# Short 32 by 32 blocks in four column strips of the tensor engine: a one-core block of attention, state-space convolution and low-rank feed-forward

## The reference

```python
def attention(h):                        # h = einsum('bct,bcd->bdt', x, W[condition])
    q, k, v = h @ Wq + bq, h @ Wk + bk, h @ Wv + bv          # 512 -> 4096
    q, k = rms_norm(q, gq), rms_norm(k, gk)                  # over all 4096
    # 32 heads of 128; the attention is within each batch of 32 tokens
    attn = softmax(einsum('bhqd,bhkd->bhqk', q, k) / sqrt(128))
    return einsum('bhqk,bhkd->bhqd', attn, v) @ Wo + bo
def ssm(u):                              # per token position (32 channels), over the 512 features
    K = 2 * einsum('hn,hnl->hl', Ct, exp(P)).real            # kernel of 512 taps for each channel
    y = irfft(rfft(u, 1024) * rfft(K, 1024))[..., :512] + u * D      # a causal convolution
    return y * (arange(512) < length)
def ffn(y):                              # 8 groups of 128 tokens, each with a gate over 16 adapters
    A_eff, B_eff = gate @ lora_A, gate @ lora_B              # rank 32, beside a shared pair
    return y @ kernel + bias + (y @ A_eff.T) @ B_eff.T + (y @ A_s.T) @ B_s.T
x = x + attention(mix(x));  return x + ffn(ssm(x))
```

## Time and profile before

| | |
|---|---|
| median of 3 runs | 891.25 us (889.63 to 892.67) |
| profiled execution | 890.15 us, its span 888.4 us |
| granted TensorE clock, mean over the span | 0.996 |
| TensorE matmuls busy | 97% of the span, 4,529 instructions |
| TensorE weight loads busy | 81% (beside the matmuls) |
| VectorE, GpSimd, ScalarE busy | 66%, 50%, 43% |

### The profile page before, as it was taken

One profiled execution on the slowest core, in us unless ns is written; L12 is line 12 of the kernel. 1 busy time (PEld: TensorE's weight loads), 2 busy tenths in 40 slices (PEclk: granted clock), 3 DMA queues, 4 the chain that ended last, 5 costly groups with the idle time before them and its releaser, 6 DMA issues.

```text
span 888.4 us, 12311 instructions
## 1 busy us (share of the span) xinstructions
PE 857.6 (97%) x4529; PEld 715.3 (81%) x4529; DVE 585.8 (66%) x641; ACT 378.5 (43%) x494; POOL 440.2 (50%) x429
## 2 busy tenths in 40 slices
PE   5799999999999999999799999999999999999988
PEld 4588888888888888888688888888888888888465
DVE  3977888887777777777856646566575766452421
ACT  3556555566555555564323214442321414132410
POOL 5989844432222222111999700469999995000500
PEclk9999999999999999999899999999999999999999
DMA  6125111111111111220011010131401011437301
GB/s 172 48 79 139 47 41 48 34 51 43 44 47 47 47 47 47 71 95 0 1 48 48 18 58 20 47 94 47 96 8 53 35 48 50 172 113 236 108 24 72
DMA packets 77473, 56.50 MB, mean 64 GB/s; under 512 B 25494, under 2 KB 60662, under 8 KB 77318
## 3 DMA queue, kind: packets, MB, share of 16 engines
q1 hardware_dynamic: 76480, 55.67, 20.8%
q10 hardware_dynamic: 966, 0.48, 0.2%
HBM read 52.32 MB, written 3.82 MB: 63 GB/s over the span
## 4 chain that ended last, share of the span: by engine, by line
PE 89%; POOL 5%; DVE 2%; ACT 1%; issue 1%; DMA 0%; ACTq 0%; POOLq 0%
PE psum L636 14%; PE psum L637 14%; PE psum L638 14%; PE psum L682 10%; PE psum L683 10%; PE psum L684 10%; PE psum L776 6%; PE psum L715 6%; PE psum L880 2%; PE psum L909 1%; PE psum L931 1%; POOL small L466 1%; POOL w_raw L401 1%; DVE wv_lo L1292 1%; POOL small L467 1%
## 5 line engine op out<-in xcount | busy, mean ns | idle before, releaser
L396 POOL TENSOR_TENSOR w_raw<-w_raw 128x256 f32<-128x256 f32 x32 | 26.7, 836 | 175.2 <-DMA w_raw<-in_wk 174.7
L1417 DVE TENSOR_TENSOR acc<-psum,acc 128x512 f32<-128x512 f32 x64 | 44.2, 691 | 96.0 <-PE psum L638 96.0
L682 PE MATMUL psum<-t_hi,w_hi 128*128 128x512 f32 x256 | 102.6, 401 | 1.9 <-DVE qk_sb L1259 0.9
L636 PE MATMUL psum<-wv_hi,mix_hi 128*128 128x512 f32 x256 | 100.3, 392 | 0.0
L683 PE MATMUL psum<-t_lo,w_hi 128*128 128x512 f32 x256 | 99.8, 390 | 0.0
L684 PE MATMUL psum<-t_hi,w_lo 128*128 128x512 f32 x256 | 99.7, 390 | 0.0
L637 PE MATMUL psum<-wv_lo,mix_hi 128*128 128x512 f32 x256 | 99.6, 389 | 0.0
L638 PE MATMUL psum<-wv_hi,mix_lo 128*128 128x512 f32 x256 | 99.6, 389 | 0.0
L1092 ACT ACTIVATE attn_hi<-psum,params 128x512 fp32r<-128x512 f32 x64 | 43.6, 688 | 116.5 <-PE psum L776 116.1
L636 PE MATMUL psum<-wo_hi,attn_hi 128*128 128x512 f32 x224 | 87.1, 389 | 0.0
L637 PE MATMUL psum<-wo_lo,attn_hi 128*128 128x512 f32 x224 | 87.1, 389 | 0.0
(11 more groups left out here) (237 smaller groups left out, 1915.4 us busy)
## 6 DMA issues: line engine op xcount, KB each, us to landing
w_raw<-in_wq SPq DMA_DIRECT2D x32, 256.0 KB, 2.9
w_raw<-in_wk SPq DMA_DIRECT2D x32, 256.0 KB, 3.2
wv_raw<-in_wv SPq DMA_DIRECT2D x8, 1024.0 KB, 5.4
toep<-kpad_dram SPq DMA_DIRECT2D x2, 4096.0 KB, 14.5
wo_raw<-in_wo SPq DMA_DIRECT2D x7, 1024.0 KB, 5.3
x_nat<-in_x SPq DMA_DIRECT2D x4, 512.0 KB, 6.0
acc<-in_x SPq DMA_DIRECT2D x1, 2048.0 KB, 10.0
out_dram<-o_stage SPq DMA_DIRECT2D x8, 256.0 KB, 2.0
```

The lines of the kernel that those rows point to most:

```text
L636: mm(out, lh, rh, start=(n == 0), stop=False)
L682: mm(bank(n), wh, hi[:, c, tok], start=(i == 0), stop=False)
L1417: v.tensor_tensor(acc[:, g, :], bank(6 + g % 2), acc[:, g, :], ALU.add).then_inc(acc_ok, 1)
```

## The change

1. The scores of a head become 32 matmuls of 32x32 instead of 8 of 128x128. Batch b of a group runs in column strip b of the array and lands on partitions 32b to 32b+31 of one half bank. `extract` becomes one copy of 128x256.
2. The second quad's value weights get tiles of their own (`wv_hi1`, `wv_lo1`). ScalarE splits them after the fifth group's copy and no longer waits for the value products; GpSimd's tables wait for sixteen value groups (`v_mm`, 2G) and no longer for `p_ok`.
3. The kernel generation goes in four strips (channel 8q+i in strip q) into one bank. The copy to `k_sb`, the load of D, the addition of D and the writing to `kpad` each become four pieces, and the addition also waits for the first half of `mix_lora`.
4. The last output weights are split before the last attend: ScalarE's high part when all value products are done, VectorE's remainder within quad 6, after the fifth accumulation.
5. The down product runs per group in two strips of 64 columns, waits for `y_t` and the adapters alone, and no longer makes the unused halves. Its result and `b_all` are split, and the up product is three f32r matmuls. ScalarE makes `y_t` ahead of `y_hi` in the last unit. GpSimd's zeroing moves behind the fourth convolution unit.

```diff
             for g in range(G):
-                last = mm(bank(6, 1024)[:, P * g:P * g + P], qk_sb[:, slot, 0, P * g:P * g + P],
-                          qk_sb[:, slot, 1, P * g:P * g + P], start=True, stop=True)
+                for b in range(BPG):
+                    tok = slice(P * g + SEQ * b, P * g + SEQ * b + SEQ)
+                    last = mm(bank(6)[quadrant(b), SEQ * g:SEQ * g + SEQ], qk_sb[:, slot, 0, tok],
+                              qk_sb[:, slot, 1, tok], start=True, stop=True, tile_position=(0, 32 * b))
...
-                for b in range(BPG):
-                    src = bank(6, 1024)[quadrant(b), :].rearrange("p (g k) -> p g k", g=G)[:, :, quadrant(b)]
-                    last = sc.activation(dst[quadrant(b), :].rearrange("p (g k) -> p g k", g=G), src, ACT.Copy)
-                last.then_inc(s_ok, 1)
+                sc.activation(dst, bank(6, G * 32), ACT.Copy).then_inc(s_ok, 1)
...
-            pool.wait_ge(p_ok, 1)
+            pool.wait_ge(v_mm, 2 * G)
...
-                value_group(1, g)
+                value_group(1, g, hi=wv_hi1, lo=wv_lo1)
...
-            for g in range(4, G):
+            value_out(0, 4)
+            act.wait_ge(wv1_in, 16)
+            sc.activation(wv_hi1[:].rearrange("p c n -> p (c n)"), wv_raw1[:].rearrange("p c n -> p (c n)"),
+                          ACT.Copy).then_inc(wvhi_ok, 1)
+            for g in range(5, G):
                 value_out(0, g)
-            act.wait_ge(wv1_in, 16)
-            act.wait_ge(v_mm, G)
-            sc.activation(wv_hi[:].rearrange("p c n -> p (c n)"), wv_raw1[:].rearrange("p c n -> p (c n)"),
-                          ACT.Copy).then_inc(wvhi_ok, 1)
...
-            split_v(1, raw=wv_raw1)
+            split_v(1, raw=wv_raw1, hi=wv_hi1, lo=wv_lo1)
...
-                last = mm(bank(0, 1024)[0:CA, CL * h:CL * h + CL], u_tab[:, :, h], expo[:, 0:CL, h],
-                          start=True, stop=True)
+                i, q = h // 4, h % 4
+                last = mm(bank(0)[32 * q:32 * q + CA, CL * i:CL * i + CL], u_tab[:, :, 8 * q + i], expo[:, 0:CL, 8 * q + i],
+                          start=True, stop=True, tile_position=(0, 32 * q))
...
-            gp.tensor_tensor(k_sb[:, :, CL - 1], k_sb[:, :, CL - 1], d_rows[:], ALU.add).then_inc(kern_d, 1)
+            pool.wait_ge(lora, 2 * NLORA - 1)
+            for q in range(4):
+                rows = slice(32 * q, 32 * q + CA)
+                gp.tensor_tensor(k_sb[rows, :, CL - 1], k_sb[rows, :, CL - 1], d_rows[rows, :], ALU.add).then_inc(kern_d, 1)
+                pool.wait_ge(kern_d, q + 1)
...
-            gp.memset(ax[:], 0.0).then_inc(ax_zero, 1)
...
+            pool.wait_ge(conv_mm, 4)
+            for tile in (ax_hi, ax_lo):
+                gp.memset(tile[:].bitcast(F32), 0.0).then_inc(ax_zero, 1)
...
-            attn_out(NQ - 1, range(4))
+            act.wait_ge(v_mm, G * NQ)
             split_o(NQ - 1, hi=wv_hi, raw=wv_raw)
-            attn_out(NQ - 1, range(4, 8))
+            attn_out(NQ - 1)
...
                     accumulate(t, (3 + c,), first)
+                    if c == 1 and not split:
+                        split_o(t + 1, hi=wv_hi, lo=wv_lo, raw=wv_raw)
...
             pe.wait_ge(yt_ok, 8)
-            pe.wait_ge(ylo_ok, 8)
             pe.wait_ge(a_in, 16)
             for j in range(G // 2):
-                down(j)
+                for c in range(KC):
+                    for k in range(2):
+                        g = 2 * j + k
+                        last = mm(bank(0)[2 * RANK * k:2 * RANK * k + 2 * RANK, P * j:P * j + P], a_all[:, c, g, :],
+                                  y_t[:, c, BPG * g:BPG * g + BPG, :], start=(c == 0), stop=(c == KC - 1),
+                                  tile_position=(0, 64 * k))
+            last.then_inc(ax_mm, 1)
+            pe.wait_ge(ylo_ok, 8)
...
-                pe.wait_ge(ax_ok, g + 1)
+                if g < 2:
+                    pe.wait_ge(axlo_ok, g + 1)
                 if g == 0:
-                    pe.wait_ge(b_in, 64)
-                mm(o, ax[:, g, :], b_all[:, g // 2, :], start=False, stop=True).then_inc(out_mm, 1)
+                    pe.wait_ge(blo_ok, 1)
+                mm(o, ax_hi[:, g, :], b_hi[:, g // 2, :], start=False, stop=False)
+                mm(o, ax_hi[:, g, :], b_lo[:, g // 2, :], start=False, stop=False)
+                mm(o, ax_lo[:, g, :], b_hi[:, g // 2, :], start=False, stop=True).then_inc(out_mm, 1)
...
+                if u == 3:
+                    act.wait_ge(b_in, 64)
+                    sc.activation(b_hi[:].rearrange("p j n -> p (j n)"), b_all[:].rearrange("p j n -> p (j n)"),
+                                  ACT.Copy).then_inc(bhi_ok, 1)
+
+            def half_groups(tile, k):
+
+                return tile[2 * RANK * k:2 * RANK * k + 2 * RANK].rearrange("p (j k) t -> p k j t", k=2)[:, k]
+
+            def low_rank(k):
+
+                return bank(0)[2 * RANK * k:2 * RANK * k + 2 * RANK, :].rearrange("p (j t) -> p j t", j=G // 2)
+
+            act.wait_ge(ax_mm, 1)
+            act.wait_ge(ax_zero, 2)
+            for k in range(2):
+                sc.activation(half_groups(ax_hi, k), low_rank(k), ACT.Copy).then_inc(axhi_ok, 1)
...
+                if u == 5:
+                    dve.wait_ge(bhi_ok, 1)
+                    v.tensor_tensor(b_lo[:].rearrange("p j n -> p (j n)"), b_all[:].rearrange("p j n -> p (j n)"),
+                                    b_hi[:].rearrange("p j n -> p (j n)").bitcast(F32), ALU.subtract).then_inc(blo_ok, 1)
             y_low(7)
...
+            for k in range(2):
+                rows = slice(2 * RANK * k, 2 * RANK * k + 2 * RANK)
+                dve.wait_ge(axhi_ok, k + 1)
+                v.tensor_tensor(ax_lo[rows].rearrange("p (j k) t -> p k j t", k=2)[:, k],
+                                bank(0)[rows, :].rearrange("p (j t) -> p j t", j=G // 2),
+                                ax_hi[rows].rearrange("p (j k) t -> p k j t", k=2)[:, k].bitcast(F32),
+                                ALU.subtract).then_inc(axlo_ok, 1)
```

More of the change, by code:

```diff
@@ L149, in build_program @@
          (wo_raw, _, wv_raw),
-         (_, wv_raw1),
+         (_, wv_hi1, wv_raw1),
+         (_, wv_lo1),
          (_, ang, expo, mult, quarter, quarter_pi),
@@ L155, in build_program @@
          (t_hi, t_lo, w_raw0, w_hi0, w_lo0, w_raw1, w_hi1, w_lo1, qk_sb, sq, sumsq, bo_rows),
-         (ffn_lo, ffn_hi, a_all, b_all, ax, fb_rows, mask, _, x2p, y_t, y_hi, y_lo),
+         (_, b_lo),
+         (ffn_lo, ffn_hi, a_all, b_all, _, fb_rows, mask, b_hi, x2p, y_t, y_hi, y_lo),
          (wo_lo, wo_hi, _, wv_lo, wv_hi, v_sb, p_blocks, attn_hi, attn_lo)) = overlay(
@@ L170, in build_program @@
              ("bo_rows", [P, FEAT], F32)],
+            [gap(24), ("b_lo", [P, G // 2, FEAT], F32R)],
             [("ffn_lo", [P, KC, FEAT], F32R), ("ffn_hi", [P, KC, FEAT], F32R), ("a_all", [P, KC, G, 2 * RANK], F32),
-             ("b_all", [P, G // 2, FEAT], F32), ("ax", [P, G, P], F32), ("fb_rows", [P, FEAT], F32),
-             ("mask", [P, FEAT], F32), gap(8), ("x2p", [P, SEQ, KC, BATCH], F32), ("y_t", [P, KC, BATCH, SEQ], F32),
+             ("b_all", [P, G // 2, FEAT], F32), gap(4), ("fb_rows", [P, FEAT], F32),
+             ("mask", [P, FEAT], F32), ("b_hi", [P, G // 2, FEAT], F32R), ("x2p", [P, SEQ, KC, BATCH], F32), ("y_t", [P, KC, BATCH, SEQ], F32),
              ("y_hi", [P, KC, BATCH, SEQ], F32R), ("y_lo", [P, KC, BATCH, SEQ], F32R)],
@@ L756, in _, with value_group @@
                     head_qk(i * 2 + j, j)
-            def value_group(t, g, free=True):
+            def value_group(t, g, free=True, hi=wv_hi, lo=wv_lo):
                 if free:
@@ L764, in value_group @@
                          [(mix_hi[:, c, P * g:P * g + P], mix_lo[:, c, P * g:P * g + P],
-                           wv_hi[:, c, :], wv_lo[:, c, :]) for c in range(KC)]).then_inc(v_mm, 1)
+                           hi[:, c, :], lo[:, c, :]) for c in range(KC)]).then_inc(v_mm, 1)
             def attend(t, first=False):
@@ L958, in _ @@
             act.wait_ge(d_zero, 1)
-            act.dma_start(d_rows[CA - 1:CA, :], every_partition(ssm_d, 32, 1)).then_inc(misc_in, 16)
+            for q in range(4):
+                act.dma_start(d_rows[32 * q + CA - 1:32 * q + CA, :],
+                              bass.AP(ssm_d.tensor, 8 * q, [[0, 1], [1, 8]])).then_inc(misc_in, 16)
             act.dma_start(bo_rows[:], every_partition(bo, FEAT)).then_inc(bo_in, 16)
@@ L1152, in _ @@
             act.wait_ge(soft, 6 * 4 + 1)
-            sc.activation(k_sb[:].rearrange("a h c -> a (h c)"), bank(0, 1024)[0:CA, :], ACT.Copy).then_inc(kern_ok, 1)
+            for q in range(4):
+                rows = slice(32 * q, 32 * q + CA)
+                last = sc.activation(k_sb[rows].rearrange("a h c -> a (h c)"), bank(0, 8 * CL)[rows, :], ACT.Copy)
+            last.then_inc(kern_ok, 1)
             with act.Fori(4, NQ - 2) as t:
@@ L1177, in _ @@
```

(18 more changed lines are left out.)

36 lines of the change are left out of this document (14 added, 22 removed).

## The result

The changed kernel takes 857.03 us (855.03 to 857.83), the kernel before 891.14: a ratio of 0.961 with an interval of 0.959 to 0.962. The profiled execution took 855.03 us, its span is 853.2; against the span before, 888.4, that is 35.2 us less where the sum said 48.5.

A forecast was written before the change was run, and what follows sets the result against it. TensorE, busy 97% of the span, was taken as the bound. Terms of -29.4, -8.8, -2.9, -1.5 and -5.9 sum to -48.5 us from 890.15: 841.6 profiled, 842 us in the runs, range 834 to 890.

The forecast's parts named there:

- the sum: Whole kernel: gains of all five parts together, -48.5 us, giving 841.6 for the profiled execution, 842 in the runs.
- rival A: Scores in the heads: strips overlap but a round costs 0.061 us; all together 35 us less, 856 us; chance 0.17.
- The price of the scores: Head loop: a round of four strips costs 0.035 us, scores take 0.92 us less a head, -29.4 us over 32 heads.
- B: Scores in the heads: at 32 columns strips follow one another, heads +8 us; 880 us (863 to 892); chance 0.18.
- C: Scores in the heads: instruction supply bounds, 0.061 us each whatever the strip; 920 to 952 us; chance 0.17.
- Is another engine the bound then?: Head loop: VectorE 88% busy at 10.4 us a head; 0.97 us of slack before w_lo's reader just covers 0.92 gain.
- rival D: Head loop: VectorE's chain is the bound, 10.6 us a head, +6, 848 us; chance 0.45 together with the forecast.
- The first attend: First attend: separate second value weights and later GpSimd tables remove its stop and the slow clock, -8.8 us.
- Kernel generation: Kernel generation: 16 rounds in four strips take 0.98 us for 3.92, -2.9 us; 0 if strided reads don't overlap.
- Last weights and tail: Output weights split before the last attend, -1.5 us; tail with earlier, stripped down product and f32r up product, -5.9 us.

The follow-up runs named there:

- part 1 alone: Kernel before with only the scores in four strips and one copy out (`head_scores`, `extract`): 875.9 us beside 891.9, ratio 0.9805.
- timed bias additions: Changed kernel with VectorE's second addition of squares in two halves and each GpSimd bias addition waiting for w_lo: 844.9 us, ratio 0.9462.

## Why the prediction was right, and where it wasn't

The time, 857, lies in the stated range of 834 to 890, but not at the 842 of the sum and not in the likeliest stretch, 834 to 852 with its chance of 0.45. It lies where rival A stood, with 0.17. That the range held owes as much to its width as to the working.

**The price of the scores** was right, from the convolution's rows. 0.035 us a round was taken; 0.034 was measured, and the early heads lie the forecast 10.4 us apart. Rival A (0.061 a round), B (strips one after the other) and C (instruction supply) all fall: one strip alone takes 0.033 us an instruction, four take 0.0084. The 60 cycles for each matmul of the Trainium skill ("TensorEngine Tiling (Array Packing)", Instruction Overhead), an estimated 25 ns at 2.4 GHz, aren't seen across strips. A single strip at 33 ns, of which 27 are its columns by the prediction's count, neither shows nor excludes them. The 62 ns per matmul that the Trainium skill gives for decoding in microcode ("TensorE: Matmul & The Clock Gate", Wait — 56ns, not 53.3ns?) aren't seen in either run.

**The step that failed** is the question "Is another engine the bound then?", answered with 0.97 us of slack for a gain of 0.92. It took VectorE's operations at the lengths that they had in a head of 11.32 us, and it read the slack at one head. Two things came in its place. A shorter head moved the second addition of squares 1 us towards the last weight sum of GpSimd, where it takes up to 0.5 us longer; from the fourteenth head on the distances are 10.7 instead of 10.4, about 4.6 us in sum. And in the heads with bias additions w_lo takes 2.4 us, which the longer heads had nearly covered before; these are 10.9 to 11.3 us apart, about 5.1 us in sum over 10.42, of which 3.4 go when the bias additions are left out. The heads came out at 10.7 on average and the term at 19.2 instead of 29.4 (first table). That is rival D, given as 10.6, with a larger price: about 10 us instead of 6. With the late start it brought the time to 857, where rival A had been put: the same number for another reason. The experiments tell them apart, since with one addition moved TensorE does keep 10.42. VectorE's share was near, 88% forecast and 87% measured, but it could not warn: an engine that is free for 13% of a head still set the pace, because its free time lies elsewhere than ahead of w_lo:

```profile
50.70:373.00 322.30, 319.03 (x3181) 251.81 (x3180) 279.88 (x303) 171.60 (x180) 139.37 (x179) 1.00 0.20 57
```

**The first attend**: both causes and the size held. GpSimd's tables ended later, at 522.7 us, and ScalarE took them up at 534.4, so 11.7 us of cover were left, for 12 forecast. **Kernel generation**: strided operands overlap in the strips too, 1.07 us for 0.98. **Last weights and tail**: -1.5 and -6.0 for -1.5 and -5.9. In the tail the down product begins 24.6 us behind the convolution's start for 25.5 before, and a group takes 3.40 us for 3.63. From its start to the next product the down product takes 3.65 us for 6.79. The prediction had compared with the record of 7.14, which holds the last matmul's tail; small misses the other way made up for it.

**Open**: why TensorE's clock falls in the start in ten of the twelve profiles, and to 0.76 or to 0.88. The wait for the low part of the mixed input is 3.1 us at 1.00 in the kernel before and 3.6 at 0.76 in the changed one, but 3.2 at 0.76 with part 1 alone and 3.5 at 0.88 with timed bias additions, so its length alone doesn't tell. No run changed it on purpose.

## What to carry to other kernels

When a stage gets shorter, recompute for every other engine not only its share of the shorter stage but which of its operations will now run beside which: here a phase that shifted by 1 us put two SBUF operations on top of each other. Read the slack in all turns of the loop and not at one: the heads beside the bias additions had 0.05 to 0.46 us where the one that was read had 0.97. Together the two cost a third of the gain. What an engine does that nobody waits for soon (here an addition of squares) belongs behind, or into the gaps of, the chain that the bounding engine waits for. And the price of a form that the trace doesn't show may be read from a row with the same form at another size, rather than from one with the same size in another form.

## What the runs showed of the hardware

f32 matmuls of 32 columns in four column strips cost 0.0084 us an instruction, measured on 64 more behind the first 64, while one strip alone gives 0.033 us each. VectorE's split of 2.0 us takes up to 3.1 us beside one GpSimd addition of 1.3, and its addition of 1.22 us takes 1.69 beside one of 0.74. A combination of VectorE that reads PSUM keeps its 0.68 us beside a GpSimd addition of 1.29.
